# Two attentions in one kernel: a table of f1 and wider row products in the first, two heads per matmul in the preparation of the second

## The chip, the cores and the metric

The kernel runs on one core of a Trainium2 chip. The metric is device time in microseconds (us) of one execution. The core has five engines with a queue each: TensorE (PE, with its weight loads listed as PEld), VectorE (DVE), ScalarE (ACT), GpSimd (POOL) and SyncE (SP, which here only issues DMAs). They meet only by semaphores.

## The reference

x has 2708 rows of 256 numbers, adj is 2708 by 2708 with entries 0 and 1. Two layers, each an attention and a feed-forward part with residuals:

```
# layer 0, attention: 4 heads of 64
support = LN(x) @ weight                       # per head
f1 = support . weight_u ;  f2 = support . weight_v
w = leaky_relu(f1[None, :] + f2[:, None], 0.2) * adj
attn = softmax over the entries where adj != 0
x = x + attn @ support + bias + LN(x) @ proj_w.T + proj_b
# layer 0, feed-forward: mixture of 16 experts, top 2
# layer 1, attention: 4 heads of 64
q, k, v = split(LN(x) @ Wqkv + bqkv)
scores = q k^T / 8 + graph_bias * adj ;  -1e9 where adj == 0
x = x + softmax(scores) @ v @ Wout + bout
# layer 1, feed-forward: 30 steps of tanh, silu, layer norm and a 256 x 256 product
```

## The kernel before

Rows are cut into NT = 22 tiles of P = 128 rows (the last overlaps its neighbour by OVER = 108 rows), taken in NPAIR = 11 pairs; a tile is (i, b), pair i and half b. The program is a sequence of phases with a barrier between them: `layer0_prepare`, `layer0_attention`, the mixture of experts (three phases), `layer1_prepare`, `layer1_attention`, `layer1_ffn`. Within a phase each engine has a list of instructions written out by hand; nothing reorders them. Names in the profile carry the phase: p_ for a preparation, a_ for an attention, m_ for the experts, f_ for the last part.

**`layer0_attention`** works in units (i, b, h): one tile of 128 rows, one head, all 2708 columns; 88 units. For each unit:

- PE (`logits`) makes fo = off + f1 in three chunks of 1024, 1024 and 660 columns. For each span of 512 columns there are two matmuls into PSUM: IDB (identity) times `off` (L656; `off` is -2^63 where adj is 0), and SEL[h] times F1P (L658). F1P holds f1 of all columns, each head split in three bf16 parts, in 12 rows; SEL[h] picks the three rows of head h. There are two chunk buffers (fo 0 and 1).
- ACT (`low_part`, L528) reads the chunk and writes low = 0.2 * fo + F2S (0.2 * f2, one number per row).
- DVE (`leaky`, L580) writes lg = max(fo + f2, low): the leaky relu. So a chunk buffer is free when ACT and then DVE have read it.
- DVE (`mask`, L591) multiplies the whole row by adj and takes the maximum, in one custom instruction; L594 negates the maximum.
- ACT (`exp_part`, L536) takes the exponential of the row and its sum.
- PE (`turn`, L671) transposes the 22 blocks of 128 columns in six groups (of 4, the last of 2) into three PSUM banks (tp); each group is copied to SBUF (`copies`, L484), groups 0, 2, 3, 4 by ACT and 1, 5 by DVE, before its bank is used again.
- PE (`weighted`, L686) multiplies the transposed rows of a pair of heads with V, 22 block products per head; ACT copies the result (L544), PE turns it back (L694), DVE adds it to X (`finish`, L616).

What sets the order: `step(unit)` in each engine's block. PE in step u transposes groups 0 to 2 of u, makes chunk 2 of the logits of unit u+2, transposes groups 3 to 5, makes chunks 0 and 1 of unit u+3, and does half a pair's `weighted`. DVE in step u does `leaky` and `mask` of u+2; ACT does the exponential of u+1. `lg` has four rows, one per head. `over_units` writes out pair 0, loops over pairs 1 to 9 in a hardware loop whose body is one pair (8 units), and writes out pair 10.

POOL makes `off` from adj (L507) and then replaces adj by adj - off in place (L513), each in four pieces, one tile at a time. adj has two buffers; SP loads the next tile into a buffer when the `mask` of head 3 has read it.

**`layer0_prepare`** ends with the table F1P: DVE splits f1 in three bf16 parts, PE turns them tile by tile (L365), and ACT and DVE cast the six groups into F1P (`f1_copies`, L241).

**`layer1_prepare`** goes tile by tile: POOL normalises (L116), PE transposes (L862), ACT copies (L827), PE multiplies with the weights (L872, L879), ACT adds the bias (L836), DVE makes the float16 parts: QT and KH are high parts (L789, L792), KL and the lower half of QT the rests (L800, L802). The weights of q and k are doubled at the start (`wqk`, L819), so that each head of 64 comes out twice, in rows 0 to 63 and 64 to 127; a matmul makes one head of one tile, 128 columns. Each float32 matmul stands as two in the trace.

Of the kernel before, what the change touches and what calls it, by code (L numbers as in the profile page):

```python
# [5 lines left out]
ALU = mybir.AluOpType  # L6
# [8 lines left out]
P = 128  # L15
# [18 lines left out]
SLOPE = 0.2  # L34
BIG = 3e38
# [118 lines left out]
def layer0_prepare(nc, io, keep):  # L154


    X, V, F12, F2S, F1P, IDB, SEL, ident, neg_half = (
        keep[n] for n in ("X", "V", "F12", "F2S", "F1P", "IDB", "SEL", "ident", "neg_half"))
    with Phase(nc, "p0") as ph:
# [6 lines left out]
        bias = ph.sb("bias", [P, 3, D])  # L166
        ones = ph.sb("ones", [P, P])
        rows_kept = ph.sb("rows_kept", [P, 1])
        hsel = ph.sb("hsel", [P, H])
        rest = ph.sb("rest", [P, 2, NT, H])  # L170
        parts = ph.sb("parts", [P, NT, H, 3], BF16)
# [11 lines left out]
         bsum, prods, masked, split, f1_turned, f1_out, sel_done, f1_clear) = ph.sems(  # L183
            "w_in uv_in cleared consts stats moments inv pchain folded wuv_done pwt_ps pwt_sb "
            "bsum prods masked split f1_turned f1_out sel_done f1_clear")
# [22 lines left out]
        def _(pool):  # L208
# [3 lines left out]
            pool.memset(F1P[:, :], 0.0).then_inc(f1_clear, 1)  # L212
# [21 lines left out]
        def f1_copies(eng, copy, first):  # L234

            eng.wait_ge(f1_clear, 1)
            for g in range(first, NG, 2):
                t0, t1 = GRP * g, min(GRP * g + GRP, NT)
                c0, c1 = t0 * P, min(t1 * P, N)
                eng.wait_ge(f1_turned, g + 1)  # L240
                copy(F1P[0:3 * H, c0:c1], turned_f1(t0, c0)[:, 0:c1 - c0]).then_inc(f1_out, 1)  # L241

        def turned_f1(t0, col):

            g = t0 // GRP
            bank = (pf, pp, pt)[g // 2]
            return bank[0:3 * H, g % 2, col - t0 * P:]

        @block.vector
        def _(dve):  # L250
# [12 lines left out]
            for j in range(2):  # L263
# [4 lines left out]
            dve.tensor_reduce(hsel[:, :], ident[:, 0:3 * H].rearrange("p (h r) -> p h r", h=H), AX.X,  # L268
                              ALU.add).then_inc(sel_done, 1)
            dve.wait_ge(sel_done, 2)  # L270
            for h in range(H):
                dve.tensor_scalar(SEL[:, h, :], ones[:, :], hsel[:, h:h + 1], None, ALU.mult).then_inc(sel_done, 1)

# [20 lines left out]

            f1 = F12[:, :, H:2 * H]
            for r in range(3):
                dve.tensor_copy(parts[:, :, :, r], f1).then_inc(split, 1)
# [72 lines left out]
        def _(act):  # L370
# [13 lines left out]
            f1_copies(act, act.copy, 0)  # L384


def later(unit, k):
# [25 lines left out]
TB = 3  # L413
# [1755 lines left out]
```

## Time and profile before

| what | before |
|---|---|
| median of three runs | 2834.41 us (2833.89 to 2835.02) |
| the profiled execution | 2834.12 us, of which its span 2832.3 us |
| busy, share of the span | PE 90%, DVE 74%, ACT 63%, POOL 53% |
| `layer0_prepare` | until about 72 us |
| `layer0_attention` | 73.6 to about 854 us |
| mixture of experts | about 855 to 1223 us |
| `layer1_prepare` | 1223.5 to about 1339 us |
| `layer1_attention`, `layer1_ffn` | from about 1340 us |

All times in the trace are counted from the span's start. The profile is read for one stage at a time: the shares of the whole span mix eight phases with different limits. "Idle before" a group of instructions is time in which its engine stood still just before it, with the work that ended the wait behind the arrow. PE's instructions overlap, so how long a stretch of its work takes is read from start to start, not from the busy times.

### The profile page before, as it was taken

What the parts mean: (1) busy time and instruction counts of PE and PEld (TensorE: products, weight loads), DVE (VectorE), ACT (ScalarE), POOL (GpSimd) and SP (SyncE); (2) the same over time, 40 slices, a digit from 0 to 9 for tenths busy, and PEclk for the clock granted to TensorE, in tenths of its full rate; (3) what the DMA queues carried; (4) which work ended last, traced back from release to release, by engine and by line L of the source; (5) the groups of instructions that cost most, each with busy time, mean ns of one, the idle gap of its engine ahead of it and who ended that gap; (6) DMA issues with size and microseconds to landing.
All of it is one profiled execution on the core that took longest, in us unless ns stands there. A gap on an engine that the chain in (4) does not pass through costs nothing. (4 is left out here: it accounts for less than half of the span.)

```text
span 2832.3 us, 61724 instructions
## 1 busy us (share of the span) xinstructions
PE 2535.5 (90%) x20690; PEld 2066.0 (73%) x20691; DVE 2105.7 (74%) x4352; ACT 1788.5 (63%) x3178; POOL 1498.9 (53%) x1753
## 2 busy tenths in 40 slices
PE   6699899989995799368899999999959999999999
PEld 5366666666674799358577777777748888888888
DVE  5799999999985444565777777777667777777776
ACT  1698888888881233244566666666647777777775
POOL 5766666666625355331212111221078888888886
PEclk9799999999995899779999999999979999999999
DMA  2011111111108222310111111111000000000001
GB/s 95 21 41 40 39 39 39 42 52 43 39 1 279 80 69 70 109 53 6 40 41 39 46 52 39 39 39 59 1 6 0 0 0 0 0 0 0 0 0 40
DMA packets 44338, 113.26 MB, mean 40 GB/s; under 512 B 6149, under 2 KB 30446, under 8 KB 38510
## 3 DMA queue, kind: packets, MB, share of 16 engines
q1 hardware_dynamic: 38702, 97.17, 9.8%
q0 software_dynamic: 5568, 15.21, 1.7%
q8 instruction: 40, 0.66, 0.1%
q14 instruction: 28, 0.23, 0.0%
HBM read 99.21 MB, written 13.15 MB: 40 GB/s over the span
## 5 line engine op out<-in xcount | busy, mean ns | idle before, releaser
L2070 PE MATMUL f_pm<-f_wl,f_yt 128*128 128x256 f32 x2640 | 625.4, 380 | 0.0
L2070 PEld LDWEIGHTS f_pm<-f_wl,f_yt 128*128 128x128 f32 x2640 | 477.2, 191 | 51.6
L507 POOL TENSOR_SCALAR a_off<-ADJ 128x677 bf16<-128x677 f32 x88 | 299.5, 3425 | 254.4 <-DMA ADJ<-in_adj 242.7
L1014 POOL TENSOR_TENSOR ADJ<-ADJ,a_off 128x2708 f32<-128x2708 f32 x22 | 131.1, 5960 | 538.0 <-DVE ADJ L1093 538.0
L116 POOL TENSOR_SCALAR f_yy<-f_th,f_rs 128x255 f32<-128x255 f32 x660 | 366.8, 570 | 21.8 <-POOL f_rs L111 21.8
L1920 DVE SCALAR_TENSOR_TENSOR f_gg<-f_th,f_pm 128x512 f32<-128x512 f32 x319 | 219.0, 687 | 173.1 <-ACT f_th L2014 172.1
L580 DVE SCALAR_TENSOR_TENSOR a_lg<-a_fo,F,a_low 128x1024 f32<-128x1024 f32 (+1 forms) x264 | 297.6, 1155 | 45.8 <-ACT a_low L528 23.5
L2014 ACT ACTIVATE f_th<-f_pm 128x512 f32<-128x512 f32 x319 | 190.5, 597 | 199.8 <-PE f_pm L2070 199.8
L1073 DVE CUSTOM_DVE_ANT_0 a_sc<-a_qk,ADJ 128x1024 f32<-128x1024 f32 (+1 forms) x264 | 288.3, 1093 | 30.6 <-PE a_qk L1171 30.6
L671 PE MATMUL a_tp<-ident,a_lg 128*128 128x128 f32 x1936 | 264.4, 278 | 46.0 <-DVE a_wt L484 45.5
L1037 ACT ACTIVATE a_sc<-a_sc,a_mx 128x1024 f32<-128x1024 f32 (+1 forms) x264 | 277.7, 1052 | 42.6 <-DVE a_mx L1078 42.6
L988 ACT COPY a_wt<-a_tp 128x512 f32<-128x512 f32 x264 | 153.9, 583 | 236.1 <-PE a_tp L1193 235.3
L528 ACT ACTIVATE a_low<-a_fo,F2S 128x1024 f32<-128x1024 f32 (+1 forms) x264 | 259.6, 1025 | 55.3 <-PE a_fo L658 53.5
L591 DVE CUSTOM_DVE_ANT_0 a_lg<-a_lg,ADJ 128x2708 f32<-128x2708 f32 x88 | 285.6, 3245 | 0.9 <-DVE a_lg L580 0.5
L671 PEld LDWEIGHTS a_tp<-ident,a_lg 128*128 128x128 f32 x1936 | 207.6, 141 | 92.8 <-DVE a_wt L484 66.2
L1193 PE MATMUL a_tp<-ident,a_sc 128*128 128x128 f32 x1936 | 261.7, 276 | 0.2
L1193 PEld LDWEIGHTS a_tp<-ident,a_sc 128*128 128x128 f32 x1936 | 215.4, 141 | 42.1 <-issue 19.4
L1927 DVE BATCH_NORM_STATS2 f_st<-f_th 128x6 f32<-128x256 f32 x660 | 245.8, 414 | 0.0
L1214 PE MATMUL a_po<-a_wt,V 128*64 128x128 f32 x3872 | 240.3, 276 | 0.0
L1214 PEld LDWEIGHTS a_po<-a_wt,V 128*64 128x64 f32 x3872 | 208.7, 137 | 41.5 <-issue 36.3
L988 DVE COPY a_wt<-a_tp 128x512 f32<-128x512 f32 (+1 forms) x264 | 158.3, 600 | 107.9 <-PE a_tp L1193 107.9
L686 PEld LDWEIGHTS a_po<-a_wt,V 128*64 128x64 f32 x3872 | 209.6, 137 | 37.3 <-issue 35.5
(284 smaller groups left out, 4969.0 us busy)
## 6 DMA issues: line engine op xcount, KB each, us to landing
ADJ<-in_adj SPq DMA_DIRECT2D x44, 1354.0 KB, 5.9
W<-in_L_ffn_w SPq DMA_DIRECT2D x32, 512.0 KB, 9.4
m_got<-YD SPq DMA_DIRECT2D x6, 768.0 KB, 10.5
out<-X SPq DMA_DIRECT2D x21, 128.0 KB
X<-in_x SPq DMA_DIRECT2D x3, 768.0 KB, 9.3
XD<-XF SPq DMA_DIRECT2D x3, 768.0 KB
m_b<-in_L_ffn_b SPq DMA_DIRECT2D x1, 2048.0 KB, 8.4
m_rows<-XD,SLOT POOLq DMA_INDIRECT x58
```

Of the source, the lines that this page charges most:

```text
L116: return eng.tensor_scalar(out, x, rs[:, 0, bass.ds(t, 1)], rs[:, 1, bass.ds(t, 1)], ALU.mult, ALU.add)
L507: pool.tensor_scalar(off[:, b, cols], adj[:, b, cols], 0.0, -HUGE, ALU.is_equal, ALU.mult).then_inc(off_done[b], 1)
L528: act.activation(low[:, s, 0:cn], fo[:, s, 0:cn], ACT.Identity, scale=SLOPE, bias=F2S[:, bass.ds(i * 2 + b, 1), h]).then_inc(low_done[s], 1)
L580: dve.scalar_tensor_tensor(lg[:, h, c0:c0 + cn], fo[:, s, 0:cn], F12[:, bass.ds(i * 2 + b, 1), h], low[:, s, 0:cn], ALU.add, ALU.max).then ...
L591: dve.tensor_tensor_reduce(lg[:, h, :], lg[:, h, :], adj[:, b, :], 1.0, -BIG, ALU.mult, ALU.max, mx[:, h, 0:1]).then_inc(masked[h], 1)
L671: mm = pe.transpose(tp[:, BANKS[g], (j - j0) * P:(j - j0 + 1) * P], lg[:, h, col:col + P], ident[:, :])
L988: copy(wt[:, (hp * NC + c) % 2, s, j - c * CT:end - c * CT, :], tp[:, bank(group), 0:(end - j) * P]).then_inc(copied[bank(group)], 1)
L1037: act.activation(sc[:, h, c0:c0 + cn], sc[:, h, c0:c0 + cn], ACT.Exp, bias=mx[:, h, NC:NC + 1], accum_out=den[:, h, c:c + 1]).then_inc(exp ...
L1073: dve.tensor_tensor_reduce(sc[:, h, c0:c0 + cn], qk[:, s, 0:cn], adj[:, b, c0:c0 + cn], 1.0, -BIG, ALU.add, ALU.max, mx[:, h, c:c + 1]).th ...
L1193: mm = pe.transpose(tp[:, bank(group), (j - j0) * P:(j - j0 + 1) * P], sc[:, h, col:col + P], ident[:, :])
L1214: mm = pe.matmul(po[s * HD:(s + 1) * HD, 0:P], V[:, j, 2 * hp + s, 0:HD], wt[:, (hp * NC + c) % 2, s, j - c * CT, :], start=(j == 0), stop ...
L2070: mm = pe.matmul(out, yt[:, g, r, k, :], wl[:, k, :], start=(k == 0), stop=(k == KD - 1))
```

## The change

In `layer0_attention` and the end of `layer0_prepare`:

- F1P becomes FP, whose rows 32 to 43 hold the parts of f1 as before, rows 64 to 75 the parts of f2 (both from one PE product per tile, 44 rows), and rows 0 to 11 hold ones. ACT makes for each tile and head a matrix ROWS (four activations of 12 by 128 per tile, `rows_of`): rows 0 to 11 hold f2 of the tile's 128 rows for that head, rows 32 to 43 pick f1. So ROWS[b, h] times FP is f1 + f2.
- `off` changes its sign: fo = f1 + f2 + 2^63 where adj is 0. adj - off is negative there, and the product in `mask` stays very negative.
- A table f1s = 0.2 * f1 (four heads by 2708, the same for all tiles) is made once at the start of the attention (`table`: 12 chunks, PE spreads, ACT and DVE copy in turn). DVE's `leaky` becomes max(f1s + F2S, fo). `low_part` and its buffer go.
- All six groups of transposed blocks are copied by ACT, none by DVE.
- `lg` has three rows (LB = 3) in place of four, taken in turn. For that the hardware loop has three pairs in its body (24 units) in place of one.
- The mask of the very first tile (`off` and adj - off) is made by DVE in place of POOL.

In `layer1_prepare`: work goes by pairs of tiles and pairs of heads. wqkv is used as it is; a matmul makes two heads (rows 0 to 63 and 64 to 127) for 256 columns. ACT adds the bias and casts the high parts (`high`), DVE makes the rests (`low`) and then copies both to their places, 12 copies of 64 rows by 2 by 256 per pair (`place`; 20 in the last pair), since both halves of QT, KH and KL are still wanted. The loops are written out. The core of the diff:

```
 def over_units(eng, step):
-    pair(0)
-    with eng.Fori(1, NPAIR - 1) as i:
-        pair(i)
-    pair(NPAIR - 1)
+    pair(0, 0)
+    with eng.Fori(0, (NPAIR - 2) // LB) as m:
+        for r in range(LB):
+            pair(m * LB + (r + 1), r + 1)
+    pair(NPAIR - 1, NPAIR - 1)
...
-        low = ph.sb("low", [P, 2, 1024])
-        lg = ph.sb("lg", [P, H, N])
+        f1s = ph.sb("f1s", [P, H, N])
+        lg = ph.sb("lg", [P, LB, N])
...
             def step(unit):
-                if later(unit, 2):
-                    low_part(later(unit, 2), 1)
-                if unit[2] % 2 == 0 and later(unit, -4):
-                    sums_out(later(unit, -4))
-                copies(act, act.copy, unit, by_act[0:2])
-                if later(unit, 2):
-                    low_part(later(unit, 2), 2)
-                if later(unit, 1):
-                    exp_part(later(unit, 1))
-                copies(act, act.copy, unit, by_act[2:])
-                if later(unit, 3):
-                    low_part(later(unit, 3), 0)
+                if unit[2] == 0 and unit.later(H):
+                    rows_of(unit.later(H))
+                copies(act, act.copy, unit, range(0, TB))
+                if unit[2] % 2 == 0 and unit.later(-4):
+                    sums_out(unit.later(-4))
+                if unit.later(1):
+                    exp_part(unit.later(1))
+                copies(act, act.copy, unit, range(TB, NG))
...
-                dve.wait_ge(low_done[s], number)
+                dve.wait_ge(fo_done[s], number)
                 dve.nop(nofuse=True)
-                dve.scalar_tensor_tensor(lg[:, h, c0:c0 + cn], fo[:, s, 0:cn], F12[:, bass.ds(i * 2 + b, 1), h],
-                                         low[:, s, 0:cn], ALU.add, ALU.max).then_inc(leaky_done[s], 1)
+                dve.scalar_tensor_tensor(lg[:, unit.turn, c0:c0 + cn], f1s[:, h, c0:c0 + cn], F2S[:, bass.ds(i * 2 + b, 1), h],
+                                         fo[:, s, 0:cn], ALU.add, ALU.max).then_inc(leaky_done[s], 1)
...
             def step(unit):
-                ahead = later(unit, 2)
+                ahead = unit.later(2)
                 if ahead:
                     leaky(ahead, 0)
                     leaky(ahead, 1)
-                copies(dve, dve.tensor_copy, unit, (1,))
-                if ahead:
                     leaky(ahead, 2)
-                copies(dve, dve.tensor_copy, unit, (5,))
...
+            quarters = [slice(k * N // parts, (k + 1) * N // parts) for k in range(parts)]
+            dve.wait_ge(adj_in[0], 16)
+            for cols in quarters:
+                dve.tensor_scalar(off[:, 0, cols], adj[:, 0, cols], 0.0, HUGE, ALU.is_equal,
+                                  ALU.mult).then_inc(off_done[0], 1)
+            table(1, 2 * NC)
+            dve.wait_ge(off_done[0], parts)
+            for cols in quarters:
+                dve.tensor_tensor(adj[:, 0, cols], adj[:, 0, cols], off[:, 0, cols], ALU.subtract).then_inc(adj_done[0], 1)
...
-                    mm = pe.matmul(fo[:, s, n0:n0 + nn], SEL[:, h, :], F1P[:, c0 + n0:c0 + n0 + nn],
+                    mm = pe.matmul(fo[:, s, n0:n0 + nn], ROWS[:, b, h, :], FP[:, c0 + n0:c0 + n0 + nn],
                                    start=False, stop=True)
...
+            def place(i):
+                pieces = [(i * W2, 0, W2)] if i < NPAIR - 1 else [(i * W2, 0, P), (i * W2 + P, P + OVER, P - OVER)]
+                done = placed if i < NPAIR - 1 else last_placed
+                for s in range(2):
+                    rows = slice(s * HD, (s + 1) * HD)
+                    heads = slice(s, H, 2)
+                    for part, j, out, r in ((high, 0, QT, 0), (high, 1, KH, 0), (high, 1, KH, 1),
+                                            (low, 0, QT, 1), (low, 1, KL, 0), (low, 1, KL, 1)):
+                        to = slice(r * HD, (r + 1) * HD)
+                        for col, c0, cn in pieces if j else [(i * W2, 0, W2)]:
+                            dve.tensor_copy(out[to, heads, col:col + cn],
+                                            part[rows, i % 2, j, :, c0:c0 + cn]).then_inc(done, 1)
```

Three places in the order. DVE in the middle of the first attention, two units' steps before (fo, low and F are the chunk, ACT's result and f2; a_wt<-a_tp is the copy of a group):

```order
L580 SCALAR_TENSOR_TENSOR a_lg<-a_fo,F,a_low 128x1024 x2
L484 COPY a_wt<-a_tp 128x512
L580 SCALAR_TENSOR_TENSOR a_lg<-a_fo,F,a_low 128x660
L484 COPY a_wt<-a_tp 128x256
L591 ISA a_lg,a_mx<-a_lg,ADJ 128x2708
L591 ISA a_mx 128x1
L594 TENSOR_SCALAR a_mx<-a_mx 128x1
L602 TENSOR_SCALAR a_rec<-a_den 128x2
L606 RECIPROCAL a_rec<-a_rec 128x2
```

and the same engine and place now:

```order
L621 SCALAR_TENSOR_TENSOR a_lg<-a_f1s,F2S,a_fo 128x1024 x2
L621 SCALAR_TENSOR_TENSOR a_lg<-a_f1s,F2S,a_fo 128x660
L632 ISA a_lg,a_mx<-a_lg,ADJ 128x2708
L632 ISA a_mx 128x1
L635 TENSOR_SCALAR a_mx<-a_mx 128x1
L642 TENSOR_SCALAR a_rec<-a_den 128x2
L646 RECIPROCAL a_rec<-a_rec 128x2
```

The two copies have left DVE's list, and the three `leaky` stand together. ACT at the same place before (the exponential is L536):

```order
L484 COPY a_wt<-a_tp 128x512 x2
L528 ACTIVATE a_low<-a_fo,F2S 128x660
L536 ACTIVATE a_lg,a_den<-a_lg,a_mx 128x2708
L484 COPY a_wt<-a_tp 128x512 x2
L528 ACTIVATE a_low<-a_fo,F2S 128x1024 x2
L544 COPY a_ot<-a_po 128x128
```

and now, with the first unit of a tile, where ROWS are made:

```order
L582 ACTIVATE ROWS<-FP,HSEL 12x128 x4
L518 REGISTER_ALU
L521 COPY a_wt<-a_tp 128x512 x3
L572 COPY a_ot<-a_po 128x128
L564 ACTIVATE a_lg,a_den<-a_lg,a_mx 128x2708
L518 REGISTER_ALU
L521 COPY a_wt<-a_tp 128x512 x2
L521 COPY a_wt<-a_tp 128x256
```

The three `low` activations are gone, and the copies of groups 3 to 5 stand behind the exponential of the next unit. DVE in the preparation of the second attention, one tile before:

```order
L789 COPY QT<-p_full 128x4x128
L792 REGISTER_ALU
L792 COPY KH<-p_full 128x4x128
L794 ISA
L794 TENSOR_TENSOR V<-p_pv,p_bv 128x4x64
L800 ISA
L800 TENSOR_TENSOR QT<-p_full,QT 64x4x128
L802 REGISTER_ALU
L802 TENSOR_TENSOR KL<-p_full,KH 128x4x128
```

and one pair of tiles now (the second half of the copies reads the other 64 rows and prints alike):

```order
L880 TENSOR_TENSOR p_low<-p_full,p_high 128x1024
L859 TENSOR_TENSOR V<-p_pv,p_bv 128x4x64 x2
L873 COPY QT<-p_high 64x2x256
L873 COPY KH<-p_high 64x2x256 x2
L873 COPY QT<-p_low 64x2x256
L873 COPY KL<-p_low 64x2x256 x2
```

The casts from float32 have become one subtraction and twelve small float16 copies per pair.

## Rows read from the trace of the kernel before

**Rows 1.** Windows view: us, busy us and count per engine, PE clock, DMA share, GB/s.

```profile
200.00:800.00 600.00, 542.26 (x5494) 408.46 (x5492) 569.03 (x699) 529.89 (x666) 397.87 (x142) 1.00 0.11 39
1240.00:1330.00 90.00, 90.00 (x738) 87.11 (x737) 51.89 (x98) 50.35 (x175) 17.06 (x29) 1.00 0.00 0
```

**Rows 2.** Waits view, 200 to 800 us: total us, times, longest.

```profile
PE a_tp L671 <- DVE a_wt L484: 38.1, 70, 0.6
...
PE a_fo L656 <- DVE a_lg L580: 19.7, 34, 0.9
```

**Rows 3.** Timeline of PE over one unit: start, duration.

```profile
804.27 1.53 PE L671 MATMUL a_tp<-ident,a_lg 128*128 128x128 f32 x12
805.63 0.45 PE L656 MATMUL a_fo<-a_off,IDB 128*128 128x512 bf16 x2
...
806.20 0.60 PE L671 MATMUL a_tp<-ident,a_lg 128*128 128x128 f32 x4
807.07 0.87 PE L671 MATMUL a_tp<-ident,a_lg 128*128 128x128 f32 x6 [0.27 <-DVE a_wt L484]
...
812.26 0.98 PE L671 MATMUL a_tp<-ident,a_lg 128*128 128x128 f32 x7
```

**Rows 4.** Groups by form, 200 to 800 us: total us, mean ns.

```profile
L591 DVE CUSTOM_DVE_ANT_0 a_lg<-a_lg,ADJ 128x2708 f32<-128x2708 f32 x70 | 229.1, 3273 | 0.4 <-issue 0.3
...
L528 ACT ACTIVATE a_low<-a_fo,F2S 128x1024 f32<-128x1024 f32 x140 | 149.7, 1132 | 0.0
...
L484 DVE COPY a_wt<-a_tp 128x512 f32<-128x512 f32 x70 | 47.7, 681 | 0.0
...
L484 DVE COPY a_wt<-a_tp 128x256 f32<-128x256 f32 x69 | 29.1, 421 | 1.5
```

**Rows 5.** Timeline of ACT in the same unit as Rows 3.

```profile
804.96 0.59 ACT L484 COPY a_wt<-a_tp 128x512 f32<-128x512 f32 x1 [0.20 <-PE a_tp L671]
...
807.16 2.54 ACT L536 ACTIVATE a_lg<-a_lg,a_mx 128x2708 f32<-128x2708 f32 x1
```

**Rows 6.** Timeline of PE: transposes of unit 1 and of unit 85 begin.

```profile
110.56 0.63 PE L671 MATMUL a_tp<-ident,a_lg 128*128 128x128 f32 x4 [0.41 <-ACT a_wt L484]
...
828.35 1.53 PE L671 MATMUL a_tp<-ident,a_lg 128*128 128x128 f32 x12
```

**Rows 7.** Tile views of off and lg: ns min/median/max, first and last start.

```profile
L507 POOL TENSOR_SCALAR a_off<-ADJ x88: 2472/2486/5280, 73.6 to 789.0; 128x677 bf16<-128x677 f32 x88
L513 POOL TENSOR_TENSOR ADJ<-ADJ,a_off x88: 1462/1480/4230, 83.5 to 798.5; 128x677 f32<-128x677 f32 x88
...
L591 DVE CUSTOM_DVE_ANT_0 a_lg<-a_lg,ADJ x88: 2966/2975/4165, 91.6 to 832.6; 128x2708 f32<-128x2708 f32 x88
```

**Rows 8.** Timeline of the first attention's start: POOL's first off, DVE's first leaky.

```profile
73.63 9.88 POOL L507 TENSOR_SCALAR a_off<-ADJ 128x677 bf16<-128x677 f32 x4 [11.67 <-POOLq L56]
...
86.79 1.28 DVE L580 SCALAR_TENSOR_TENSOR a_lg<-a_fo,F,a_low 128x1024 f32<-128x1024 f32 x1 [14.40 <-ACT a_low L528]
```

**Rows 9.** DMA view, 140 to 240 us; then 250 to 790 us, with loads (us to landing).

```profile
q8 instruction: 7, 0.11, 0.5%
...
q1 hardware_dynamic: 2304, 22.18, 11.4%
...
ADJ<-in_adj SPq DMA_DIRECT2D x16, 1354.0 KB, 5.9
```

**Rows 10.** Timeline of PE over one tile of the second attention's preparation.

```profile
1296.10 1.95 PE L872 MATMUL p_pk<-p_xt,p_wqk 128*128 128x128 f32 x16
1297.89 1.03 PE L879 MATMUL p_pv<-p_wqkv,p_xt 128*128 128x256 f32 x4
1298.76 0.38 PE L862 MATMUL p_pt<-ident,p_xn 128*128 128x128 f32 x2
```

**Rows 11.** Tile view of full, with DVE: ns min/median/max, first and last start.

```profile
L792 DVE CAST KH<-p_full x22: 406/407/626, 1239.5 to 1336.7; 128x512 f32 x20, 128x512 f16<-128x512 f32 x2
...
L802 DVE TENSOR_TENSOR KL<-p_full,KH x22: 692/693/694, 1240.9 to 1338.2; 128x512 f32 x20, 128x512 f16<-128x512 f32 x2
```

More of the change, by code:

```diff
@@ L559, in _, with rows_of @@
-            for h in range(2):
-                for c in range(NC):
-                    low_part((0, 0, h), c)
-            exp_part((0, 0, 0))
-            low_part((0, 0, 2), 0)
+            def rows_of(unit):
+                i, b, h = unit
+                if unit.later(-H - 1):
+                    s, number = chunk(unit.later(-H - 1), NC - 1)
+                    act.wait_ge(fo_done[s], number)
+                act.nop(nofuse=True)
+                for k in range(H):
+                    act.activation(ROWS[0:3 * H, b, k, :], FP[F2ROW:F2ROW + 3 * H, bass.ds((i * 2 + b) * P, P)],
+                                   ACT.Identity, scale=HSEL[F2ROW:F2ROW + 3 * H, k:k + 1]).then_inc(rows_done[b], 1)
@@ new lines, in step, with table @@
+                if unit.later(3):
+                    logits(unit.later(3), 0)
+                    logits(unit.later(3), 1)
+                if first_of(unit).later(-2):
+                    weighted(first_of(unit).later(-2), 0 if even else 1)
+            def table(first, end):
+                for n in range(first, end):
+                    if n >= first + 2:
+                        pe.wait_ge(f1s_done[n % 2], n // 2)
+                    elif first:
+                        pe.wait_ge(leaky_done[n % 2], NC)
+                    c0, cn = CHUNKS[n % NC]
+                    for n0 in range(0, cn, 512):
+                        nn = min(512, cn - n0)
+                        mm = pe.matmul(fo[:, n % 2, n0:n0 + nn], SEL[:, n // NC, :], FP[:, c0 + n0:c0 + n0 + nn],
+                                       start=True, stop=True)
+                    mm.then_inc(spread[n % 2], 1)
+                for s in range(2):
+                    pe.wait_ge(f1s_done[s], end // 2)
@@ new lines, in results @@
+            def results(i):
+                dve.wait_ge(high_done, i + 1)
+                if i >= 2:
+                    dve.wait_ge(placed, (i - 1) * PLACES)
+                dve.tensor_tensor(low[:, i % 2, :, :, :], full[:, i % 2, :, :, :], high[:, i % 2, :, :, :],
+                                  ALU.subtract).then_inc(low_done, 1)
+                values(i, 0)
+                values(i, 1)
+                dve.wait_ge(low_done, i + 1)
+                place(i)
+            for i in range(NPAIR):
+                results(i)
@@ L852, in _ @@
+            turned_out(0)
+            for i in range(NPAIR):
+                if i < NPAIR - 1:
+                    turned_out(i + 1)
+                full_out(i)
         @block.tensor
@@ L897, in chunk_groups @@
+            turn(0)
+            for i in range(NPAIR):
+                if i < NPAIR - 1:
+                    turn(i + 1)
+                product(i)
 def chunk_groups(c):
```

420 lines of the change are left out of this document (210 added, 210 removed).

## The prediction

> **What bounds the kernel now.** The change touches two stages, so I read each by itself. For the first attention I took the windows view from 200 to 800 us [rows 1]: DVE is busy 569 of 600 us, PE 542, ACT 530, POOL 398. The groups view of the same stretch counts 70 masks [rows 4], so a unit takes 600 / 70 = 8.57 us. DVE at 95% is the bound; PE is close behind, and the waits view says for what PE stands still: 38.1 us for a transpose bank that DVE has yet to copy (in every one of the 70 units) and 19.7 us for a chunk buffer that DVE has yet to read [rows 2]. Both are DVE. From the start of unit 1's transposes to those of unit 85 there are (828.35 - 110.56) / 84 = 8.545 us per unit [rows 6]; this is the pace that I multiply.
>
> The preparation of the second attention is different. There PE is busy for all of the 90 us from 1240 to 1330, with DVE and ACT below 60% [rows 1]: it is bound by PE's matmuls.
>
> **The first attention, per unit.** *DVE* loses the two copies: 47.7 + 29.1 us in 70 units [rows 4], 1.10 us each unit. Its `leaky` has the same form and sizes (three chunks, one operand in PSUM, one in SBUF), so I leave it at its price; it now waits for PE alone, not for PE and then ACT. Busy 569.0 / 70 = 8.13 becomes 7.03. Before, 0.44 us of idle per unit came on top; I keep half of it, for the waits from one instruction to its successor in the same unit: 7.25, bounds 7.03 and 7.47.
>
> *PE* does the same matmuls in number and size. What does one unit cost it without the waits? In the timeline, unit to unit is 812.26 - 804.27 = 7.99 us; four transposes start at 806.20, and the next six only at 807.07, where four take 4 x 1.36 / 12 = 0.45 us at the pace of the twelve from 804.27 to 805.63. The stall is 0.42 us, and PE's own work 7.57 us [rows 3]. The other way round: (600 - 38.1 - 19.7) / 70 = 7.75 us [rows 1, 2, 4], which is too high, as the idle shown (0.27) is less than the stall by starts. So the floor of PE is 7.5 to 7.6 and lies above the 7.25 of DVE: **PE becomes the bound, just**. As the mask varies between 2.97 and 4.17 us [rows 7], DVE will at times be over PE's 7.57, with some 0.8 us of lead in the two chunk buffers to swallow it. I take 7.75 us per unit; bounds 7.55 (nothing lost) and 8.2 (below). The gain is 84 x (8.545 - 7.75) = **67 us**.
>
> *ACT* loses the three `low` (149.7 us for the 1024-wide ones [rows 4], another third or so for the 660-wide), about 2.9 us a unit by starts, and gains two copies of up to 0.59 [rows 5], about 0.9 us, and a quarter of the four small activations for ROWS. No 12-row activation is in the trace; at no more than a 512-wide copy each, 0.59, they are at most 0.6 us a unit and hidden: ACT goes from 530 / 70 = 7.57 to some 6 us. But it now holds all banks, and the copies of groups 3 to 5 are queued behind the exponential, which waits for DVE's maximum. Who waits for that is PE, at the first transpose of the next unit. Counted from the start T of a unit's transposes: copy of group 0 starts at T + 0.69 [rows 3, 5], three copies end at T + 2.3, the exponential with its sum at T + 5.1, group 3 is out at T + 5.7. PE wants the bank at T + 7.75. Two microseconds of slack: costed at nothing, and DVE's maximum of that unit was ready a step earlier.
>
> *Three rows of lg in place of four*: a row is held from DVE's `leaky` (about T - 0.8) to the last transposes two units later (T + 2 x 7.75 + 3.1), 19.4 us, and comes round after 3 x 7.75 = 23.3. Nothing. *POOL*: see the rival below. *The start*: today the first logits wait for POOL's off, 9.88 us from 73.63 on, and DVE's first `leaky` starts at 86.79 [rows 8]. Now DVE makes off (a mask reads the same 2708 columns in 2.97 us [rows 7], so at most 3; I take 2), but six chunks of the table come before the first logits, each a PE chunk and a copy of some 1.1 us like `low` [rows 4], two in flight, some 7.5 us, and then adj - off by DVE, about 3 us like a mask. That gives 87 again. The other six chunks stand before DVE's mask of unit 1, 5 to 6 us later than now for PE, of which ACT's earlier exponential gives most back. Sum +2 us, bounds -3 and +6. *End of the preparation before it*: ACT casts eight groups of 12 by 512 in place of three, at the half microsecond of a copy, +2.8; DVE's wider splits +0.5.
>
> *The longer loop.* The body of PE's loop is three times as long. Instruction packets: seven on queue q8 from 140 to 240 us, none of any instruction queue from 250 to 790 us [rows 9], so today's body is fetched once and then kept. A body three times as long may have to be fetched each time round, with two backward jumps to code that is gone. Nothing in the trace prices a jump to code not held; I put 1 us in the sum and 0 to 10 in the range. The Trainium skill, "Runtime: NRT & Kernel Launch", section "Instruction fetch mechanics", says that PE holds 2048 instructions and that a taken branch outside the present window stalls for a fetch. It speaks against this part of the change; it gives no time for the stall, the trace agrees so far as its one small loop body is not fetched again, and 20 us per jump would be needed to matter.
>
> **The second attention's preparation, per pair of tiles.** *PE today*: 16 matmul records of 128 columns in 1297.89 - 1296.10 = 1.79 us, 0.112 each; four of 256 columns in 0.87, 0.218 each; two transposes, at 0.11 like the records of 128 columns, 0.22 [rows 10]. A tile is 2 x 1.79 + 0.87 + 0.22 = 4.67 us, a pair 9.3. *PE then*: 16 records of 256 columns for q and k, 8 for v, 4 transposes: 24 x 0.218 + 0.44 = 5.67 us. *DVE then*: one subtraction of 1024 (512 wide it is 0.69 [rows 11]; between that and twice that; by 1 ns a column 1.25), two additions for V as today, 0.8 together, and twelve copies of 64 rows by 512 float16 numbers. No float16-to-float16 copy is in the trace. The nearest row is the cast to KH, also 512 wide, at 0.41 [rows 11]; by starts it takes about 0.33. From below 0.2 (the source is half as wide), from above 0.45. I take 0.33, 4.0 us for twelve. DVE: 1.25 + 0.8 + 4.0 = 6.1 us per pair, bounds 4.5 and 7.5. So the bound moves from PE to DVE: 6.1 in place of 9.3. DVE starts its results near 1241 instead of 1239.5, since the first pair must be whole, and ends 11 x 6.1 = 67 us later, at 1308; today its last subtraction ends at 1338.9 [rows 11]. Gain **30 us**; with 5.67 from PE 35, with 7.5 from DVE 15. ACT per pair: four activations of 256, one cast of 1024 and one copy of 512, near 3.2 us, hidden.
>
> The Trainium skill, "VectorE: DVE Perf Modes", section "The TRN2 errata", has a measured 16-bit copy of 2048 columns at 693 ns, of which about 150 cycles are fixed. An estimate from that page is 278 cycles, 0.29 us, for 512 columns. By it DVE would need 5.55 us and PE would stay the bound, which makes the time 5 us less than my sum. By the cast row it is DVE.
>
> **The sum.** 2834.1 (the profiled execution, 0.3 under the median of the runs) - 67 - 30 + 2.8 + 0.5 + 2 + 1 = 2743.4; on the median **2744 us**.
>
> **Rivals.**
> - *DVE stays the bound in the first attention.* POOL and DVE read the same memory: POOL's pieces take from 2.5 to 5.3 us, masks from 2.97 to 4.17 [rows 7]. If masks lengthen as the units get denser, or the two-chunk lead doesn't swallow the long ones, a unit takes 8.2 and the gain is 29: 2782. For it speaks how near the two bounds are; against it that the mean mask is 3.27 with POOL busy two thirds of the time [rows 1, 4].
> - *Placing costs more*: twelve copies at 0.45 that don't overlap, since they change partitions each time. 7.5 us per pair: 2759.
> - *Better than the sum*: PE runs at its floor of 7.57 and placing is cheap: 84 x 0.18 = 15 and 5 us less: 2724.
> - *Slower than before: POOL's chain.* An adj buffer goes round as mask of head 3, load (5.9 us [rows 9]), off (four pieces), adj - off (four pieces), mask of head 0 two tiles on. With unit time x this needs 8x - 3x - 3.3 of room. The chain is 5.9 + 22.7 = 28.6 us now, from POOL's 398 us in 17.5 tiles [rows 1], and fits x = 6.4. If all pieces went to their longest, 4 x 5.28 + 4 x 4.23 [rows 7], it would be 44 and x = 9.5: 84 x 0.95 + 6.3 - 30 = +56 us, 2890. It decides from a chain of 41 us (x = 8.83). Against it: the medians, 2.49 and 1.48, are at the minimum, and DVE's share of time in masks rises only from 38 to 42%.
> - *The change doesn't do what it says*, with DVE's `leaky` slower by about what the copies cost (the operands are swapped, the table is larger): gain of the first stage gone, 2805 to 2830.
>
> **How the numbers follow.** Forecast 0.55; DVE still the bound 0.19; dear placing 0.12; better 0.06; no gain in the first attention 0.04; slower 0.04. A measurement of this kernel can tell 0.2%, 5.7 us, from no change. Faster by more: 0.94; within: 0.02; slower: 0.04. The range 2722 to 2785 holds the first four.
>
> **What would show it.** In the changed profile: DVE busy near 93% and PE near 97% between 200 and 700 us; unit pace 7.75 by the starts of PE's transposes; PE's wait for a copied bank gone, since ACT does it; waits of DVE for PE's chunk (`leaky` <- fo) in their place; masks still about 3.3 us in the mean. First transposes at 101 to 106 us. In the second preparation PE not quite full, DVE over 90%, 11 rounds of 6.1 us. It is wrong if `leaky` takes more than 1.3 us, if PE waits for ACT, if instruction packets come with gaps on PE, or if a placing copy is far from 0.33 us.

## The result and the profile after

The changed kernel takes **2735.52 us** (median of four runs, 2733.80 to 2736.17), the kernel before 2834.72 (four runs, 2833.89 to 2835.99): ratio 0.9645, 95% interval 0.9634 to 0.9656. The forecast was 2744, the range 2722 to 2785. The profiled execution has a span of 2732.0 us against 2832.3.

Where the 100.3 us went, by the same events in both traces:

| event | before | after | difference so far |
|---|---|---|---|
| first attention begins | 73.63 | 76.28 | +2.65 |
| transposes of unit 1 begin | 110.56 | 113.33 | +2.77 |
| transposes of unit 85 begin | 828.35 | 765.56 | -62.79 |
| last turn back of the first attention | 853.01 | 789.16 | -63.85 |
| `layer1_prepare`: VectorE's first instruction | 1224.02 | 1160.69 | -63.33 |
| second attention: VectorE's first instruction | 1343.00 | 1242.63 | -100.37 |

So 84 units gave 65.6 us and the preparation of the second attention 37.0; all else together lost 2.3. A unit now takes (765.56 - 113.33) / 84 = 7.765 us, before 8.545 [rows 6].

The windows view of the changed kernel (us, busy us and count of PE, PEld, DVE, ACT, POOL, then PE clock, DMA share, GB/s), to be held against [rows 1]:

```profile
200.00:700.00 500.00, 482.58 (x5032) 374.83 (x5031) 458.20 (x514) 369.49 (x610) 348.99 (x129) 1.00 0.13 46
1180.00:1230.00 50.00, 50.00 (x249) 44.14 (x248) 43.87 (x135) 27.38 (x53) 16.61 (x20) 1.00 0.00 1
```

PE went from 90 to 97% of the first stretch, DVE from 95 to 92%, ACT from 88 to 74%. The waits view of 200 to 700 us (total us, times, longest), against [rows 2]:

```profile
POOL a_off L544 <- DMA ADJ<-in_adj: 151.0, 16, 12.8
ACT a_wt L521 <- PE a_tp L730: 129.7, 64, 3.7
DVE a_lg L621 <- issue: 20.1, 49, 3.5
PE a_fo L715 <- DVE a_lg L621: 11.9, 18, 0.7
PE a_tp L730 <- issue: 5.3, 2, 2.8
```

PE's wait for a copied bank is gone; its wait for a chunk buffer that DVE has yet to read is smaller, and left in 18 of 64 units; new are two stalls of PE on nothing but issue. DVE's groups by form in the same stretch (total us, mean ns | idle before), against [rows 4]:

```profile
L632 DVE CUSTOM_DVE_ANT_0 a_lg<-a_lg,ADJ 128x2708 f32<-128x2708 f32 x64 | 209.3, 3270 | 8.4 <-DVE a_lg L621 7.7 <-issue 0.5
L621 DVE SCALAR_TENSOR_TENSOR a_lg<-a_f1s,F2S,a_fo 128x1024 f32<-128x1024 f32 x129 | 159.5, 1277 | 24.0 <-issue 20.1 <-PE a_tp L730 3.9
```

The mask has its old mean of 3.27 us, `leaky` its old 1.28. PE's transposes over three units (timeline), and its one wait in them, against [rows 3]:

```profile
251.82 1.53 PE L730 MATMUL a_tp<-ident,a_lg 128*128 128x128 f32 x12
...
259.22 1.53 PE L730 MATMUL a_tp<-ident,a_lg 128*128 128x128 f32 x12
...
266.75 1.53 PE L730 MATMUL a_tp<-ident,a_lg 128*128 128x128 f32 x12
269.00 0.46 PE L715 MATMUL a_fo<-a_off,IDB 128*128 128x512 bf16 x2 [0.72 <-DVE a_lg L621]
...
275.04 1.53 PE L730 MATMUL a_tp<-ident,a_lg 128*128 128x128 f32 x12
```

A tile's four units take 7.4, 7.5, 8.3 and 7.5 us, in this order over and over: the one from 266.75 to 275.04 is the long one, and in it PE waits 0.72 us for DVE's `leaky`. DVE was late because of the second of these masks, during which POOL subtracted (timelines of DVE and of POOL):

```profile
255.16 2.98 DVE L632 CUSTOM_DVE_ANT_0 a_lg<-a_lg,ADJ 128x2708 f32<-128x2708 f32 x1 [0.24 <-DVE a_lg L621]
263.08 4.13 DVE L632 CUSTOM_DVE_ANT_0 a_lg<-a_lg,ADJ 128x2708 f32<-128x2708 f32 x1
```
```profile
262.91 5.64 POOL L550 TENSOR_TENSOR ADJ<-ADJ,a_off 128x677 f32<-128x677 f32 x2
```

4.13 us, not 2.98, and 5.64 us for two subtractions whose median is 1.48 each [rows 7]: they hold each other up.

The preparation of the second attention, one pair of tiles on DVE (timeline), against [rows 11]:

```profile
1183.03 1.23 DVE L880 TENSOR_TENSOR p_low<-p_full,p_high 128x1024 f16<-128x1024 f32 x1 [0.37 <-ACT p_high L921]
1184.18 0.75 DVE L859 TENSOR_TENSOR V<-p_pv,p_bv 128x256 f32<-128x256 f32 x2
1184.84 0.27 DVE L873 COPY QT<-p_high 64x512 f16<-64x512 f16 x1
1185.04 0.60 DVE L873 COPY KH<-p_high 64x512 f16<-64x512 f16 x2
1185.56 0.28 DVE L873 COPY QT<-p_low 64x512 f16<-64x512 f16 x1
1185.87 0.60 DVE L873 COPY KL<-p_low 64x512 f16<-64x512 f16 x2
1186.50 0.29 DVE L873 COPY QT<-p_high 64x512 f16<-64x512 f16 x1
...
1188.65 1.25 DVE L880 TENSOR_TENSOR p_low<-p_full,p_high 128x1024 f16<-128x1024 f32 x1 [0.49 <-ACT p_high L921]
```

A round is 1188.65 - 1183.03 = 5.62 us and ends in a wait for ACT; PE is busy 50.00 of 50 us. The bound is PE; `places_more` below tests it.

### The profile page after: what moved, and what is told of

It is laid out like the page before. It is cut to its first block and busy times, and to the rows that moved or that the text cites. A ratio compares the mean times of both kernels' runs of the same rounds, so it can differ in the third digit from the quotient of the medians.

```text
span 2732.0 us, 59677 instructions
## 1 busy us (share of the span) xinstructions
PE 2485.0 (91%) x20186; PEld 2025.9 (74%) x20187; DVE 2026.6 (74%) x4258; ACT 1612.4 (59%) x3050; POOL 1481.3 (54%) x1747
## 5 line engine op out<-in xcount | busy, mean ns | idle before, releaser
L544 POOL TENSOR_SCALAR a_off<-ADJ 128x677 bf16<-128x677 f32 x84 | 275.0, 3296 | 224.2 <-DMA ADJ<-in_adj 209.6
L521 ACT COPY a_wt<-a_tp 128x512 f32<-128x512 f32 x528 | 256.3, 565 | 173.0 <-PE a_tp L730 172.8
L621 DVE SCALAR_TENSOR_TENSOR a_lg<-a_f1s,F2S,a_fo 128x1024 f32<-128x1024 f32 (+1 forms) x264 | 289.7, 1150 | 28.8 <-issue 22.7
L1061 ACT COPY a_wt<-a_tp 128x512 f32<-128x512 f32 x264 | 153.9, 583 | 236.5 <-PE a_tp L1266 235.7
L730 PE MATMUL a_tp<-ident,a_lg 128*128 128x128 f32 x1936 | 244.8, 275 | 5.9 <-issue 5.3
L564 ACT ACTIVATE a_lg<-a_lg,a_mx 128x2708 f32<-128x2708 f32 x88 | 226.6, 2575 | 12.6 <-DVE a_mx L635 12.1
```

The source lines that it names most:

```text
L521: copy(wt[:, h // 2, h % 2, j:end, :], tp[:, BANKS[g], 0:(end - j) * P]).then_inc(copied[BANKS[g]], 1)
L544: pool.tensor_scalar(off[:, b, cols], adj[:, b, cols], 0.0, HUGE, ALU.is_equal, ALU.mult).then_inc(off_done[b], 1)
L621: dve.scalar_tensor_tensor(lg[:, unit.turn, c0:c0 + cn], f1s[:, h, c0:c0 + cn], F2S[:, bass.ds(i * 2 + b, 1), h], fo[:, s, 0:cn], ALU.add, ...
L1061: copy(wt[:, (hp * NC + c) % 2, s, j - c * CT:end - c * CT, :], tp[:, bank(group), 0:(end - j) * P]).then_inc(copied[bank(group)], 1)
```

## Experiments

Ratios are to the kernel before, run beside it, with 95% intervals. "Pace" is us per unit from the transposes of unit 1 to those of unit 85.

| kernel | us | ratio | pace |
|---|---|---|---|
| changed | 2735.52 | 0.9645 (0.9634 to 0.9656) | 7.765 |
| a0_alone | 2773.57 | 0.9779 (0.9764 to 0.9794) | 7.759 |
| p1_alone | 2802.98 | 0.9879 (0.9864 to 0.9894) | 8.545 |
| copies_back | 2786.73 | 0.9820 (0.9805 to 0.9835) | 8.361 |
| act_copies | 2823.30 | 0.9958 (0.9944 to 0.9972) | 8.424 |
| pool_small | 2718.77 | 0.9590 (0.9574 to 0.9606) | 7.568 |
| no_off_products | 2721.84 | 0.9598 (0.9582 to 0.9614) | 7.640 |
| both_small | 2692.79 | 0.9495 (0.9480 to 0.9509) | 7.268 |
| places_more | 2744.80 | 0.9680 (0.9664 to 0.9696) | |
| unrolled | 2725.54 | 0.9609 (0.9596 to 0.9622) | 7.629 |
| before_unrolled | 2811.22 | 0.9912 (0.9899 to 0.9926) | 8.235 |
| before_pool_small | 2809.07 | 0.9902 (0.9885 to 0.9918) | 8.220 |
| act_negates | 2719.87 | 0.9589 (0.9576 to 0.9602) | 7.567 |

### The two parts one by one

`a0_alone` is the changed kernel with the old `layer1_prepare`, `p1_alone` the kernel before with the new one.

> The first attention's part with the second attention's preparation as before. Theory: the two parts are independent. The traces give 63.9 us at the end of the first attention (853.0 to 789.2) and 37 between the start of the second preparation and the second attention; so this is 2835 - 63 = 2772 us, and with the other part alone the gains add up to 99. Rival: the parts help each other through fetched code, memory or the clock; then the two gains miss 99 by more than 3 us.

> The kernel before with the changed preparation of the second attention alone. Theory: 2835 - 37 = 2798 us. By my working before the result it would be 2805 (DVE bound, 6.1 us a pair).

The gains are 2.21% and 1.21%, together 3.42% against 3.55% for the whole: they add up within the intervals, and the paces are those of the kernels that the first attention was taken from. Within that the two parts are independent, as expected.

### Which part of the first attention gives the gain

`copies_back` gives DVE its two copies again, and keeps the table:

```diff
                     leaky(ahead, 1)
-                    leaky(ahead, 2)
+                copies(dve, dve.tensor_copy, unit, (1,))
+                if ahead:
+                    leaky(ahead, 2)
+                copies(dve, dve.tensor_copy, unit, (5,))
```

> The changed kernel with the copies of groups 1 and 5 on DVE again, in the places where they stood before. Theory: DVE's load decides. 458.2 / 64 = 7.16 us a unit plus 1.1 for the copies is 8.26, with 0.2 to 0.4 idle 8.5; 84 x (8.5 - 7.77) = 61 more, 2797 us (2782 to 2802). Rival: the gain comes mostly from the chain chunk, low, leaky that is one engine shorter, whoever copies: then at most 20 more, below 2755.

Its waits view, 200 to 700 us:

```profile
PE a_tp L733 <- DVE a_wt L521: 30.8, 58, 0.6
```

PE waits for DVE's copy in nearly every unit again (58 waits in some 60 units), and DVE is busy 467.90 of 500 us. 2786.73 us lies in the 2782 to 2802 of the theory on the load, nearer to its lower end, and far from the rival's 2755. `act_copies` is the other half alone: the kernel before, all six copies by ACT, `low` kept.

> The kernel before with all six copies by ACT, and nothing else of the change: ACT still makes low, DVE's leaky still waits for it. Theory: the copies can leave DVE only because the table frees ACT; ACT had 7.57 us a unit and gets 1.0 more, 8.6, and with the idle it had 8.8 to 9.0: 20 to 38 us more than before, ratio 1.007 to 1.013. Rival: DVE was the bound, its relief counts more than ACT's load: 8.2 to 8.5 us a unit, ratio 0.99 to 1.00.

Here my theory missed: 0.4% faster, where I had expected about 1% slower. Its windows view:

```profile
200.00:700.00 500.00, 448.55 (x4623) 342.33 (x4679) 425.81 (x478) 480.97 (x685) 311.27 (x119) 1.00 0.12 42
```

ACT is full (96%), as expected, and DVE is down to 85%; but a unit costs ACT 480.97 / (500 / 8.424) = 8.10 us, and not 8.6. I had priced the two copies by their durations, and copies in a row overlap (in the kernel before one takes 0.59 us, two in a row 1.06): before, ACT had 440.66 us in the same stretch, 7.53 a unit, so two copies added 0.57. So the copies alone bring 0.12 us a unit, the rest of the change without them 0.18 (the table, and with it the three rows and the longer loop, whose jumps alone cost 0.07 a unit, see below), both together 0.78. Each alone runs into the next engine: ACT without the table, DVE without the move.

### What is the bound now

`pool_small` takes POOL out of the way: from the third tile on its pieces shrink to 4 columns, so later masks aren't renewed.

```diff
-                    cols = slice(k * N // parts, (k + 1) * N // parts)
+                    cols = slice(k * N // parts, k * N // parts + 4)
```

> The changed kernel, but from the third tile on POOL's eight pieces per tile are 4 columns wide and not 677, so the masks of later tiles are not renewed (the output is not the reference's). In the changed kernel one unit in four takes 8.3 us, the others 7.4 to 7.55, and in each tile one mask on DVE takes 4.1 us, not 2.97, while POOL subtracts. Theory: that is POOL and DVE in each other's way; with POOL idle all masks take 2.97, all units 7.4 to 7.55, pace 7.77 to 7.57 with the loop's jumps, 17 us less: ratio to the kernel before 0.9585. Rival: the long unit is PE waiting once per tile for the next tile's operands; then less than 5 us, ratio above 0.963.

As the theory says: pace 7.568 (expected 7.57), every unit outside the loop's jumps 7.4 to 7.6, and each mask 2.98 in the groups view:

```profile
L632 DVE CUSTOM_DVE_ANT_0 a_lg<-a_lg,ADJ 128x2708 f32<-128x2708 f32 x66 | 196.5, 2978 | 8.9 <-DVE a_lg L621 8.0 <-issue 0.8
```

`no_off_products` takes PE's share instead, and `both_small` both:

```diff
-                for n0, nn in spans:
-                    pe.matmul(fo[:, s, n0:n0 + nn], IDB[:, :], off[:, b, c0 + n0:c0 + n0 + nn], start=True, stop=False)
```

> The changed kernel without the six products with the identity that add the off values to the logits (the output is not the reference's). PE loses 5 x 0.216 + 0.06 = 1.14 us a unit, from 7.47 to 6.33; DVE's 7.16 us of work stays. Theory: PE is the bound and DVE the next: pace 7.2 to 7.4, so 31 to 48 us less, ratio 0.948 to 0.954. Rival: DVE already sets the pace and PE's fullness is a coincidence: less than 10 us, ratio above 0.961. Second rival: the chain exponential, transposes, copies is the bound: also nearly nothing.

> The changed kernel with both cuts: POOL's pieces 4 columns wide from the third tile on, and no off products on PE (the output is not the reference's). POOL's cut alone gave a pace of 7.57 us a unit, PE's alone 7.64. Theory: each alone leaves the other in charge, PE with 7.45 and DVE with some 7.5 when POOL disturbs it; with both cut DVE undisturbed is left, 449 / 66 = 6.80 busy and 0.3 idle: 7.1 to 7.2 with the loop's jumps, ratio 0.945 to 0.949. Rival: a closed chain through the three rows of lg (leaky, mask, exponential, transposes, leaky) takes 7.5 us a unit whatever the engines' loads: ratio 0.957 to 0.960.

Without the products PE has 1.1 us less in each unit, and only 0.125 of it shows: 7.640, where I had expected 7.2 to 7.4, and a ratio of 0.9598, between my 0.954 and the 0.961 of the rival that DVE already sets the pace. The waits of no_off_products and then of both_small, 200 to 700 us:

```profile
PE a_fo L715 <- DVE a_lg L621: 75.7, 65, 2.1
DVE a_lg L621 <- PE a_tp L728: 13.2, 25, 3.4
```
```profile
PE a_fo L715 <- DVE a_lg L621: 53.1, 68, 1.2
DVE a_lg L621 <- PE a_tp L728: 17.8, 40, 3.6
```

PE now waits for DVE in every unit: the next bound lies 0.125 us below the pace, not 0.4 as I expected. With both cut the pace is 7.27, a little over my 7.1 to 7.2, ratio 0.9495 where I had 0.945 to 0.949. The chain through the three rows of `lg` as a floor of 7.5 is refuted. Nor do the 17.8 us that the view puts down to PE's transposes come from it. These are lines of both_small (timelines of PE and of DVE):

```profile
259.84 1.25 PE L728 MATMUL a_tp<-ident,a_lg 128*128 128x128 f32 x10
```
```profile
265.54 3.29 DVE L621 SCALAR_TENSOR_TENSOR a_lg<-a_f1s,F2S,a_fo 128x1024 f32<-128x1024 f32 x3 [0.33 <-PE a_tp L728]
287.29 3.29 DVE L621 SCALAR_TENSOR_TENSOR a_lg<-a_f1s,F2S,a_fo 128x1024 f32<-128x1024 f32 x3 [0.27 <-issue]
```

The transposes that free the row for the `leaky` at 265.54 ended at 261.1, over 4 us before. The idle time before the first `leaky` of a unit is 0.23 to 0.33 us in every unit, whether the view calls it issue or PE, but for the loop's two jumps (3.59 and 3.27, inside the 17.8). So of the 0.57 us that DVE is idle per unit in both_small some 0.27 are this wait, 0.10 the jumps and 0.12 a wait of the mask for the `leaky` in front of it. What the first wait is, the part on the loop says.

The changed kernel thus stands where two bounds nearly meet. With the loop's jumps in both, PE alone needs 7.57 (pool_small; 7.45, the mean of 7.4 and 7.5, without the jumps), and DVE with POOL beside it 7.64 (no_off_products). Taking from either alone gives at most 0.2 us a unit, taking from both 0.5.

### The second attention's preparation

`places_more` adds four copies of the placing kind per pair:

```diff
+                        if j == 0:
+                            dve.tensor_copy(more[to, i % 2, s, :, :], part[rows, i % 2, j, :, :])
```

> The changed kernel with four more copies of the placing kind per pair of tiles on DVE (16 in place of 12; they go to a buffer that nothing reads). DVE's work rises from 5.15 to 6.2 us per pair, PE's stays 5.62. Theory: PE sets the pace of the second preparation and DVE's 0.47 us of waiting per pair is slack: 11 x 0.55 = 6 us more, ratio 0.9666. Rival: DVE's wait is a latency that it has whatever its load: 11 x 1.05 = 11.5 us more, ratio 0.9686. By my working before the result (0.33 us each and DVE bound) 14.5 more.

The time can't tell 0.9666 from 0.9686, the timeline of DVE can:

```profile
1194.61 1.22 DVE L883 TENSOR_TENSOR p_low<-p_full,p_high 128x1024 f16<-128x1024 f32 x1
1200.85 1.23 DVE L883 TENSOR_TENSOR p_low<-p_full,p_high 128x1024 f16<-128x1024 f32 x1
1207.09 1.23 DVE L883 TENSOR_TENSOR p_low<-p_full,p_high 128x1024 f16<-128x1024 f32 x1
```

6.24 us a round, and no wait in it: the first 0.5 us of added work disappeared in DVE's slack, the rest shows. PE is the bound of the changed kernel here, with DVE 0.5 us below it. That the wait is a latency (6.66 us a round) is refuted.

### The loop

PE's two stalls on issue lie 24 units apart (timeline):

```profile
354.48 1.53 PE L730 MATMUL a_tp<-ident,a_lg 128*128 128x128 f32 x12 [2.53 <-issue]
542.64 1.53 PE L730 MATMUL a_tp<-ident,a_lg 128*128 128x128 f32 x12 [2.77 <-issue]
```

The longer body is fetched anew (DMA view of the changed kernel, 250 to 790 us), where the kernel before showed no instruction packet [rows 9]:

```profile
q8 instruction: 48, 0.79, 0.6%
q14 instruction: 30, 0.25, 0.1%
```

`unrolled` writes the changed kernel's units out, `before_unrolled` those of the kernel before:

```diff
-    with eng.Fori(0, (NPAIR - 2) // LB) as m:
-        for r in range(LB):
-            pair(m * LB + (r + 1), r + 1)
+    for n in range(1, NPAIR - 1):
+        pair(n, n)
```

> The changed kernel with the 88 units of the first attention written out, no loop. Theory: PE's two stalls on nothing but issue, 2.5 and 2.8 us at 354 and 542 us, are the loop's two jumps back; written out they go, and the time is 2735.5 - 5 = 2730 us. Rival A: the stalls are fetches of code as such and come also in straight code, in more places: 2735 or more. Rival B: DVE's own loop stalls as long at the same places, and it has them in straight code too: 2735.

> The kernel before with its loop of nine pairs of tiles in the first attention written out, and nothing of the change. Its loop shows no stall on issue at the jumps and next to no instruction packets. Theory: a held body costs nothing at its jumps, only DVE's small waits on issue (8.0 us in 500, 0.2 each) can go: 0 to 10 us less, ratio 0.9965 to 1.0. Rival: straight code has to be fetched, 18 packets in 200 us, and makes it slower: above 1.001.

The theory of unrolled held for the stalls, but the gain was twice its size: 84 x 0.136 = 11.4 us. Each of the two places costs 2.9 us (9.99 + 8.01 + 8.18 and 10.23 + 7.98 + 7.97 for three units that elsewhere take 7.40 + 7.56 + 8.30), 6 in all; most of the other 5 is the long unit, 8.3 us in the loop and 8.12 written out. It goes with DVE's small waits before the first `leaky` of a unit: 24.0 us in the groups view above, 17.2 of them outside the jumps or 0.27 a unit, against 3.4 in all in unrolled, which has the same three rows of `lg`. The mean mask even rose, from 3.27 to 3.36. That the stalls are the fetch itself no run shows; unrolled shows that they go with the jumps. And before_unrolled contradicts me outright: 25 us faster. That kernel's loop is fetched once [rows 9], and PE has no stall like the two above. Written out, it fetches all the time (DMA view of before_unrolled, 250 to 790 us):

```profile
q8 instruction: 41, 0.67, 0.5%
q14 instruction: 19, 0.16, 0.1%
```

Fetching straight code costs next to nothing here (the longest wait on issue before a `leaky` is 0.4 us, once); a loop that is held does cost. What the loop has, and the written-out form has not, is work of DVE's sequencer (line view of `leaky`, kernel before: ns min/median/max, first and last start; then its idle time, us and times), and the same line in before_unrolled:

```profile
L580 DVEq FUSED_REGOPS  x72: 57/68/93, 170.5 to 779.2; - x72
...
  issue: 11.1, 55
```
```profile
  issue: 0.4, 1
```

That is one register computation per unit of the loop, in front of a `leaky` that addresses by the loop's number, and 0.2 to 0.3 us of idle with it: 8.2 us in 42 waits on issue between 200 and 700 us, and 7.2 in the other 16 units, which the view puts down to PE's transposes; 3.1 us in all when written out. Among the 16 are the jumps back of DVE's own loop (timeline of DVE, kernel before):

```profile
307.43 2.48 DVE L580 SCALAR_TENSOR_TENSOR a_lg<-a_fo,F,a_low 128x1024 f32<-128x1024 f32 x2 [0.76 <-PE a_tp L671]
376.13 2.48 DVE L580 SCALAR_TENSOR_TENSOR a_lg<-a_fo,F,a_low 128x1024 f32<-128x1024 f32 x2 [0.76 <-PE a_tp L671]
444.85 2.48 DVE L580 SCALAR_TENSOR_TENSOR a_lg<-a_fo,F,a_low 128x1024 f32<-128x1024 f32 x2 [0.76 <-PE a_tp L671]
```

Such a wait of 0.75 to 0.84 us comes every 68.7 us, once per turn of the loop's 8 units. DVE's account of the gain is: idle 0.45 us a unit before and 0.27 written out, busy 8.10 and 7.96, together the 0.31 that were measured. The busy time falls because the mean mask is 3.28 us before and 3.10 written out: in the new rhythm POOL's subtractions meet fewer masks. Why the rhythm shifts I have not shown. Nor is the register computation shown as the cause by a run of its own: none keeps the loop and drops it, and the other engines have loops too. How much POOL could cost at most is told by `before_pool_small`, pool_small's edit in the kernel before with its loop:

> The kernel before, loop kept, with POOL's pieces 4 columns wide from the third tile on (the output is not the reference's). Writing its loop out gave 26 us, and there the mean mask was 3.10 us in place of 3.28 and DVE's waits on issue were gone. Theory: before the change DVE was the bound, so every microsecond of POOL's disturbance is paid: the mask falls to 2.98, 0.30 us a unit and 25 us in all, and a little more as the small operations behind the mask are no longer held: ratio 0.989 to 0.992. The same cut in the changed kernel gave 0.20 us a unit, as PE covers part of it. Rival: the 26 us were the loop's and hardly POOL's; the loop's waits stay and the cut gives under 15 us, ratio above 0.995.

It gave 0.325 us a unit, as expected, and the loop's waits stayed: 16.5 us in 61 waits on issue before `leaky`, 0.27 each, now in every unit. The same cut in the changed kernel gives 0.197, though its masks lose as much (3.27 to 2.98). Where DVE is the bound each microsecond is paid, where PE needs nearly as much as DVE two thirds.

### A further step

`act_negates` is `unrolled` with the negated maximum made by ACT:

```diff
-                act.wait_ge(neg_max[h], tiles(unit))
+                act.wait_ge(masked[h], tiles(unit))
+                act.activation(mx[:, h, 1:2], mx[:, h, 0:1], ACT.Identity, scale=-1.0).then_inc(neg_max[h], 1)
+                act.wait_ge(neg_max[h], tiles(unit))
```

> The written-out form with one small step more: ACT, which is busy three quarters of the time, negates the maximum that its exponential needs (before it DVE did, 0.15 us and a wait on its own mask, 0.24 us a unit by starts). Theory: in the written-out form one unit in four takes 8.12 us, not 7.5, because DVE with POOL's disturbance is late; 4 x 0.24 us less on DVE takes up the 0.62: pace 7.63 to 7.48 to 7.55, 7 to 12 us less than written out alone, ratio 0.957 to 0.9585. Rival: DVE's lateness comes from the one mask of 4.1 us, and what DVE gains elsewhere it has no place to bank, with two chunk buffers: ratio 0.960 to 0.961.

2719.87 us, against 2725.54 written out alone; the kernel before took 2836.51 beside the one and 2838.66 beside the other. It is the fastest form here that computes everything. The long unit shrank from 8.12 to 7.8 us, but another grew from 7.5 to 7.58; the pace 7.567 is just outside the 7.48 to 7.55 I gave, and the intervals of the two ratios overlap, so only the traces tell the two apart.

## Why the prediction was right, and where it was not

**The first attention's pace** was forecast at 7.75 and is 7.765. The mechanism, "PE becomes the bound, just", is borne out in part only. PE sets three units of four, and DVE, late once per tile, the fourth; taken by itself DVE (7.64, no_off_products) does not need less than PE (7.57, pool_small). That the pace came out so near is luck: two terms under it were off and cancelled. PE's floor is 7.45, not 7.57: the one unit that I had measured is of the 7.5 kind, and its stall is 0.49 us, not 0.42. And DVE was put at 7.25 with bounds 7.03 and 7.47. In no_off_products its busy time is 7.06, as forecast (7.03), but its idle time 0.58 and not 0.22. The step that failed there is "I keep half of it": the wait before each unit's first `leaky`, 0.27, goes with the loop and stayed whole; the mask, in every second unit, now waits for the `leaky` right in front of it, 0.13 in the mean, where a copy stood between them before (act_copies has it too); the loop's jumps add 0.10. I also took POOL's disturbance as part of a mean mask of 3.27 us, when it comes in one mask of 4.1 us per tile, which a lead of two chunks can't swallow; it is worth 0.20 us a unit (pool_small). My allowance of 0.18 us over the floor stood for units in which DVE is late; over the true floor it is 0.32, of which 0.07 are the jumps.

**ACT** is hidden, as said: 74% busy, and the waits view has no wait of PE for its copies. So the copies behind the exponential cost nothing. **Three rows of lg** cost nothing that shows, as said: the 3.9 us that a view puts down to them are DVE's wait before `leaky` under another name. No run has four rows with the rest of the change. **POOL's chain** did not become the bound: POOL still waits for its load in each tile.

**The start.** Preparation +2.65 (I had 3.3), start of the attention +0.1 (I had 2, bounds -3 and +6). The first transposes came at 107.84, outside my 101 to 106: the table did put unit 0 6.2 us behind. What I left out is that units 0 and 1 are then done in one run, 5.49 us for the first, since most of what they need is ready; before it was 8.92.

**The longer loop** cost 6 us at its two jumps, not 1; the bounds held. Instruction packets with gaps on PE, which I had named as a sign of being wrong, did come; the sum could bear them. Where I was wrong is the thought behind it, that today's loop is free. It costs the kernel before 26 us, and the changed one 11. With both written out the change is worth 84 x (8.235 - 7.629) = 51 us in this stage; the other 15 of the 65.6 are loop cost that it is spared. The Trainium skill, "Runtime: NRT & Kernel Launch", section "Instruction fetch mechanics", says that a taken branch to code outside the window stalls for a fetch, and that kernels therefore prefer unrolling. The trace agrees with both, with 2.5 and 2.8 us for PE's two stalls and a gain in both kernels when they are written out. The loop before the change, whose body was held, is not the case that this rule speaks of, and it is the dearer one here.

**The second preparation.** PE's 5.67 us a pair is 5.62. The step that failed is the price of a placing copy, 0.33 us by starts from the cast row: six of them take 1186.50 - 1184.84 = 1.66 us, 0.28 each, the twelve 3.3 us. DVE has 5.62 - 0.49 = 5.13 us of work, PE stays the bound, and the gain is 37 us in place of 30. The Trainium skill, "VectorE: DVE Perf Modes", section "The TRN2 errata", gave an estimate of 0.29 us and by it 5 us less than my sum. The trace agrees with it: the median placing copy is 0.28 us. I should have trusted it over a row whose operation reads twice the bytes.

**The mask and POOL.** The 4.1 us masks agree with the Trainium skill, "SBUF — State Buffer", section "Who interferes with whom": a VectorE instruction with two inputs in SBUF contends with a GpSimd instruction that reads SBUF. `leaky`, which has one input in PSUM, stays at 1.28 us with and without POOL's work, and the mask falls from 3.27 to 2.98.

**The rivals.** "DVE stays the bound" was half true: in one unit of four, and the pace stayed far from its 8.2. "Placing dear" is refuted, "better" came in by its second half (placing cheap), which is most of the 8.5 us between forecast and result. "No gain" and "POOL's chain" did not happen.

## What to carry to other kernels

Two moves that each gain little (0.12 and 0.18 us a unit) can gain 0.78 together, when each alone only makes the next engine the bound: cost them against all engines of the stage at once. Where two bounds are close, look at the longest instances and at their rhythm, not at the mean: a mask that takes 1.2 us longer once per tile sets one unit in four. A wait that a view puts down to an engine is worth a look at when that engine was done: here it had been done for 4 us. Try a hand-written-out form of a loop early: it gave 0.4% to 0.9% here, most in the kernel whose bound was DVE.

## What the hardware showed that was not expected

A jump back over a body of 24 units, which is fetched anew, stalls PE for 2.5 and 2.8 us; over a body of 8 units, which is not, PE has no stall and VectorE waits 0.75 to 0.84 us. Instruction fetches for straight code (41 packets in 540 us on one queue, 19 on another) leave VectorE one wait on issue of 0.4 us before a `leaky`, and PE some of 0.2. In a loop a register operation of some 68 ns and 0.2 to 0.3 us of idle stand in front of the VectorE instruction whose address depends on the loop's number; written out, both are gone. An activation of 12 partitions by 128 takes ScalarE 0.38 us, four in a row 1.26. Float16 copies of 64 rows by 512 follow each other in 0.20 to 0.31 us even as source and target change partitions.
